# A vision tower on one core: the value-bias product moved behind the repeated values, the engines' order changed at the first LayerNorm and the gates, expert 1 split during attention

## The reference

```python
h = (tokens - mean) * rsqrt(var + eps) * gamma + beta; h = h @ w + b   # patches of 5 shifted images
n = layernorm(h)
q, k, v = n @ qkv_w.T + qkv_b                  # 12 heads of 16
a = softmax(where(mask, q @ k.T / 4, -inf))    # keys j % 8 == 0, j == i, j == i - 1, all causal
h = h + (a @ v) @ out_w.T + out_b
n = layernorm(h)
top_w, top_i = top_k(softmax(n @ router_w.T), 2)
h = h + sum_e gate_e * (gelu(n @ w1[e] + b1[e]) @ w2[e] + b2[e])   # 8 experts, hidden width 768
```

## Time and profile before

| | us |
|---|---|
| median of 3 runs | 223.51 (223.41 to 223.8) |
| profiled execution, its own time | 224.47 |
| its span, first to last instruction | 222.7 |
| PE busy | 193.5 (87%) |
| DVE busy | 139.2 (62%) |
| ACT busy | 115.8 (52%) |
| POOL busy | 78.5 (35%) |

### The profile page before, as it was taken

How to read it: one execution, slowest core, us unless ns; L and a number is a source line. 1 busy time by engine, 2 the same in 40 slices (tenths; PEclk the granted TensorE clock), 3 DMA queues, 4 the chain that set the end, 5 groups by cost and what they waited for, 6 DMA issues and landing times.

```text
span 222.7 us, 3426 instructions
## 1 busy us (share of the span) xinstructions
PE 193.5 (87%) x1124; PEld 169.9 (76%) x1124; DVE 139.2 (62%) x304; ACT 115.8 (52%) x204; POOL 78.5 (35%) x90
## 2 busy tenths in 40 slices
PE   0899988854899958878869999999999999999991
PEld 0898578743897734767759889898998989999981
DVE  4299875747422877645992766466674665756544
ACT  2297642121313123128953767968678696784620
POOL 7781006214400064110841543635436344460000
PEclk9996996955559995559996999999999999999999
DMA  6999992000530000000016008053160520000002
GB/s 139 250 306 294 225 249 53 0 0 0 150 102 0 0 0 0 0 4 0 0 55 195 0 10 236 0 143 104 31 216 0 167 80 0 0 3 0 0 0 74
DMA packets 13930, 17.20 MB, mean 77 GB/s; under 512 B 2303, under 2 KB 10112, under 8 KB 13918
## 3 DMA queue, kind: packets, MB, share of 16 engines
q1 hardware_dynamic: 13374, 17.02, 28.3%
q10 hardware_dynamic: 544, 0.03, 0.2%
HBM read 16.66 MB, written 0.39 MB: 77 GB/s over the span
## 4 chain that ended last, share of the span: by engine, by line
PE 62%; DVE 15%; SPq 8%; issue 6%; DMA 4%; ACT 3%; POOL 1%; DVEq 0%; ACTq 0%; POOLq 0%
PE ps L367 30%; PE ps L1072 15%; PE ps L1074 7%; DMA stage<-in_L_ffn_w 4%; DVE big_r L1138 3%; SPq L398 2%; DVE oh L1138 2%; PE ps L915 2%; DVE norm L1297 1%; PE ps L959 1%; PE ps L804 1%; ACT big_r L328 1%; SPq L352 1%; DVE shifted L1142 1%; POOL rs L512 1%
## 5 line engine op out<-in xcount | busy, mean ns | idle before, releaser
L367 PE MATMUL ps<-big_r,wsplit 128*128 128x512 f32 (+1 forms) x250 | 64.6, 395 | 0.0
L1138 DVE TENSOR_TENSOR big_r<-early,big_r 128x512 fp32r<-128x512 f32 x48 | 45.7, 957 | 26.1 <-ACT big_r L328 25.2
L1072 PE MATMUL ps<-wsplit,big_r 128*128 128x384 f32 x192 | 57.6, 359 | 2.6 <-DVE big_r L1138 2.6
L367 PEld LDWEIGHTS ps<-big_r,wsplit 128*128 128x128 f32 x250 | 44.3, 195 | 6.8
L1074 PE MATMUL ps<-wsplit,big_r 128*128 128x192 f32 x192 | 48.4, 252 | 0.0
L720 ACT ACTIVATE early<-ps,b1t 128x512 f32<-128x512 f32 x48 | 32.7, 682 | 29.6 <-PE ps L367 29.6
L1072 PEld LDWEIGHTS ps<-wsplit,big_r 128*128 128x128 f32 x192 | 36.4, 190 | 5.3 <-DVE big_r L1138 3.5
L1074 PEld LDWEIGHTS ps<-wsplit,big_r 128*128 128x128 f32 x192 | 36.8, 192 | 1.4
L328 ACT ACTIVATE big_r<-early 128x512 fp32r<-128x512 f32 x48 | 30.5, 635 | 1.5
L1487 DVE SCALAR_TENSOR_TENSOR t_a<-ps,gates,merge 128x192 f32<-128x192 f32 x32 | 11.8, 409 | 15.1 <-PE ps L1074 15.1
L310 POOL TENSOR_TENSOR wsplit<-stage,wsplit 128x768 fp32r<-128x768 f32 x4 | 7.4, 1843 | 31.3 <-DVE wsplit L1138 16.3
(11 more groups left out here) (220 smaller groups left out, 292.4 us busy)
## 6 DMA issues: line engine op xcount, KB each, us to landing
stage<-in_L_ffn_w SPq DMA_DIRECT2D x4, 576.0 KB, 5.6
early<-in_L_ffn_w SPq DMA_DIRECT2D x4, 576.0 KB, 5.6
shifted<-in_L_tok_w SPq DMA_DIRECT2D x6, 288.0 KB, 9.1
early<-in_x SPq DMA_DIRECT2D x3, 512.0 KB, 6.8
stage<-in_L_ffn_w SPq DMA_DIRECT2D x4, 384.0 KB, 3.4
stage<-in_L_ffn_w SPq DMA_DIRECT2D x8, 192.0 KB, 4.3
early<-in_L_ffn_w SPq DMA_DIRECT2D x4, 384.0 KB, 3.4
early<-in_L_ffn_w SPq DMA_DIRECT2D x8, 192.0 KB, 4.4
```

Of the source, the lines that this page charges most:

```text
L367: mm = nc.tensor.matmul(dst, lhs, rhs, start=(n == 0), stop=(n == 4))
L1072: nc.tensor.matmul(ps[:, AB[t], 0:2 * D], g_hi[:, j % NG, tok], w2c, start=(f == 0), stop=False)
L1138: return nc.vector.tensor_tensor(o, a, b, op)
```

## The change

- `NTB` becomes (6, 5): group 0 of the first LayerNorm is transposed into bank 6, whose last reader is the second weight piece, so PE waits there for `s_watlo` 2 in place of 4. The wait for 4 stands behind it, ahead of the Q products.
- The three value-bias products go from ahead of the first transposes to behind `repeated_v(3)`, into bank `ATB[1]`. `const_row` on DVE goes behind `outputs(1)`, and PE waits for it ahead of the transposes of `ao` of group 1. `hb` on POOL goes behind the near values.
- DVE at the first LayerNorm: the last low weight piece ahead of `less_mean(1)`, and `embedding(1)` ahead of `low_parts(0)`. ACT: the high parts of expert 0's W2 behind the high part of group 0. POOL: the low part of expert 0's W2 waits for `s_nlo` 2, the low parts of both groups.
- `strided_scores`: first the four products with 128 rows, then the four with 64.
- Expert 1's weights: ACT takes their high parts between the `previous` and `token_major` copies of attention; POOL makes W1's low parts behind `hb`, ahead of the second LayerNorm's `rstd`, and W2's low part behind it. `pair(0)` is written out ahead of the loop without that split, on ACT and DVE.
- Gates on DVE: `two_largest` ahead of `low_hidden(0, 0)`, `gate_values` behind `low_hidden(0, 3)`.

```diff
-        NTB, QB, KB, VB, SB = (5, 6), 7, 6, (0, 2, 3, 5), (6, 7)
+        NTB, QB, KB, VB, SB = (6, 5), 7, 6, (0, 2, 3, 5), (6, 7)
...
             rstd(0, 1)
+            pool.wait_ge(s_nlo, G)
             split_low_w2(pool, 0, 0)
-            pool.wait_ge(s_row, 1)
...
             near_values(0)
             near_values(1)
+            pool.wait_ge(s_nv, G)
+            pool.wait_ge(s_row, 1)
+            pool.wait_ge(s_h, TT)
+            pool.wait_ge(s_watps, 4)
+            nc.gpsimd.tensor_tensor(hb[:], h[:], const_row[:, :].unsqueeze(1).broadcast_to([P, TT, D]),
+                                    ALU.add).then_inc(s_hb, 1)
+            split_low_w1(pool, 1, 1)
             rstd(1, 0)
             rstd(1, 1)
+            split_low_w2(pool, 1, 1)
...
-            split_low(pool, 1, 1)
...
             previous(0)
+            act.wait_ge(s_emb, G + 1)
+            act.wait_ge(d_stage[1], 16 * STAGE_DMAS)
+            split_high(1, 0)
+            split_high(1, 1)
             token_major(2)
             previous(1)
             token_major(3)
             previous(2)
+            split_high(1, 2)
+            split_high(1, 3)
             previous(3)
...
+            pe.wait_ge(s_watlo, 2)
             transposes(0, n1, s_n, lambda t: t + 1, NTB, s_nt, s_ndup)
+            pe.wait_ge(s_watlo, 4)
+            pe.wait_ge(s_wathi, 5)
...
             repeated_v(2)
             repeated_v(3)
+            pe.wait_ge(d_bqk, 16 * BQK_DMAS)
+            pe.wait_ge(s_prev, TT)
+            for n, (col, part) in enumerate(((0, 0), (0, 1), (1, 2))):
+                mm = nc.tensor.matmul(ps[:, ATB[1], 0:D], bias_v[:, col:col + 1].broadcast_to([P, P]),
+                                      wat[:, part, OUT0:OUT0 + D].bitcast(F32), start=(n == 0), stop=(n == 2))
+            mm.then_inc(s_vbias, 1)
...
+            transposes(0, ao, s_ao, lambda t: t // 2 + 1, ATB, s_at, s_aodup)
+            pe.wait_ge(s_row, 1)
+            transposes(1, ao, s_ao, lambda t: t // 2 + 1, ATB, s_at, s_aodup)
...
             outputs(1)
+            dve.wait_ge(s_vbias, 1)
+            tt(const_row[:], ps[:, ATB[1], 0:D], outb_row[:], ALU.add).then_inc(s_row, 1)
...
+                        if first and slot == 0 and j == LAG:
+                            gate_values()
```

More of the change, by code:

```diff
@@ L678, in _ @@
             high_parts(0, s_nt, NTB, nt, s_nhi)
+            split_high(0, 2)
+            split_high(0, 3)
             last_columns_again(0, 1, n1)
@@ L711, in _, with pair @@
             nc.scalar.activation(table_in[:], neg_half[:, 0:1], ACT.Gelu)
-            def pair(i, last):
+            def pair(i, last, first=False):
                 for j in range(2 * FC):
@@ L723, in pair @@
                     copy(g_hi[:, j % NG], gf[:, j % NG]).then_inc(s_ghi, 1)
-                    if last and slot == 1:
+                    if last and slot == 1 or first and slot == 0:
                         continue
@@ L731, in pair @@
                         split_high(1 - slot, f - 1)
-            with act.Fori(0, E // 2 - 1) as i:
+            pair(0, False, first=True)
+            with act.Fori(1, E // 2 - 1) as i:
                 pair(i, False)
@@ L996, in strided_scores @@
                                      kbd_a[:, b].rearrange("p g j -> p (g j)"), start=True, stop=True)
+                for b in range(4 * g, 4 * g + 4):
+                    tok = slice(b * S, (b + 1) * S)
+                    rows = slice(b % 2 * S, (b % 2 + 1) * S)
+                    c0 = b // 2 % 2 * HEADS * NK
                     mm = nc.tensor.matmul(ps[rows, SB[g], c0 + 64:c0 + 96], qt[0:REM, 1, tok],
@@ L1034, in _ @@
                 mm.then_inc(s_pv, 1)
-            for g in range(G):
-                transposes(g, ao, s_ao, lambda t: t // 2 + 1, ATB, s_at, s_aodup)
+            transposes(0, ao, s_ao, lambda t: t // 2 + 1, ATB, s_at, s_aodup)
+            pe.wait_ge(s_row, 1)
+            transposes(1, ao, s_ao, lambda t: t // 2 + 1, ATB, s_at, s_aodup)
             for g in range(G):
@@ L1314, in _ @@
             normalised(0, 0, h, n1)
+            small_low_parts((3,))
             less_mean(1)
-            small_low_parts((3,))
+            embedding(1)
             low_parts(0, s_nhi, NTB, nt, s_nlo)
-            embedding(1)
             statistics(0, 1, h, s_h, lambda t: t + 1)
             normalised(0, 1, h, n1)
-            dve.wait_ge(s_vbias, 1)
             dve.wait_ge(d_rows, 16 * 2)
-            tt(const_row[:], ps[:, UB, 0:D], outb_row[:], ALU.add).then_inc(s_row, 1)
             low_parts(1, s_nhi, NTB, nt, s_nlo)
@@ L1513, in _ @@
             low_hidden(0, 2)
-            gate_values()
-            with dve.Fori(0, E // 2 - 1) as i:
+            pair(0, False, first=True)
+            with dve.Fori(1, E // 2 - 1) as i:
                 pair(i, False)
```

20 lines of the change are left out of this document (3 added, 17 removed).

## The result

The changed kernel takes 208.09 us (median of 4 runs, 206.31 to 208.92) against 223.46 in the runs beside it, a ratio of 0.930 (95% interval 0.924 to 0.936): 15.4 us less, where 11.0 were forecast, and outside the forecast's range at its low end. The profiled execution took 207.82 us, its span is 206.1 (222.7 before).

A forecast was written before the change was run, and what follows sets the result against it. The prediction saw the winnable time ahead of the expert loop at 121 us, in chained waits and PE's slow clock. Its terms summed to -11.0 us, from a median of 223.51 to 212.5 us, range 209.8 to 216.6.

The forecast's parts named there:

- Scores: Reordering of sixteen short products, twice, while PE is the bound: 0.2 us less, from nothing to 0.4.
- First LayerNorm: Reordered steps and W2's wait let tile 0's products start 5.8 us earlier, bounds 5.0 and 6.3.
- The clock in Q, K, V: PE's clock comes up near the start of tile 0: 3.1 us less, bounds 0 and 3.5.
- Value bias: Its 1.16 us hide in PE's wait for value blocks; `const_row` delays group 1's transposes by 0.15 us (0 to 0.4).
- Expert 1's split: On POOL around the second LayerNorm: W1 adds 0.5 us (bound 1.6), W2 beside the norms 0.75 (0 to 1.5).
- The clock at the router: The wait ahead of the second transposes delays the clock's rise: 0.8 us more, bounds 0 and 1.6.
- Gates: Both PE waits go, 2.6 us, and the slow stretch at 117.2, 1.5 us; bounds together 2.0 and 4.2.
- Rivals 1, 3 and 4: In order: clock no earlier, 215.6 us, chance 0.22; gates keep a wait, 216.6 us, 0.12; attention products slow, 226.1 us, 0.04.
- Rival 2: The clock also stays up from 83 us: 2.5 us less, 210.0 us; chance 0.12.

The follow-up runs named there:

- w2_no_wait: The changed kernel without POOL's wait for both low parts ahead of expert 0's W2: 212.04 us.
- s_new_on_before: The kernel before with the new order of the scores' products and nothing else: 218.28 us against 221.28, ratio 0.982.
- w2_late: The changed kernel with one wait added on POOL, so that expert 1's W2 starts behind the second LayerNorm's last norm: 206.03 us.
- ln_only: The kernel before with the first LayerNorm's edits alone (banks, value bias, `const_row`, `hb`, engine order there): 213.22 us against 222.06, ratio 0.964.
- s_old_order: The changed kernel with the scores' products in the old order, 128 rows and 64 rows in turns: 210.28 us.
- s_halves_in_turn: The changed kernel with scores' products alternating column halves, the number of rows changing at six of seven steps: 209.62 us.
- s_rows_together: The changed kernel with the scores' four 128-row products first, then the four of 64 rows, images in order 0, 2, 1, 3: 207.95 us.
- gates_only: The kernel before with expert 1's split in attention, the new order at the gates and the written-out first pair alone: 218.09 us against 222.06, ratio 0.981.
- filled: The changed kernel with expert 1's W1 low parts ahead of the near values, W2's behind the last norm, and sixteen unread products in PE's waits: 205.32 us.

## Why the prediction was wrong

- **The step that failed is "Scores".** It took the value products as the nearest row, looked for the gain in alternating column halves, and put 0.2 us with an upper end of 0.4. The four orders show that the halves are worth nothing and the change between 128-row and 64-row products 0.20 us each; taken away six times in each of two groups on a stretch where PE is the bound, this is 2.4 us. With the other terms as they came, 0.2 us here would have given 210.3 us, inside the range. The upper bound was wrong as well: it took the pace of products whose shapes do not alternate for that of products whose shapes do, and no row of the scores themselves was read for it: in the trace of the kernel before their sixteen records of 64 and 32 columns took 1.95 us a group, where eight records of 192 columns took 0.87 us for the values at the same clock (80.63).
- **First LayerNorm: right.** -6.0 for -5.8, by the steps named: transposes 2.6 us ahead of the first low part, norms at 0.67. `w2_no_wait` shows 2.2 of it to be W2's wait.
- **The clock in Q, K, V: right in place and size.** -3.2 for -3.1, tile 0 at 1.73 us. In all eleven profiled executions with the new first LayerNorm the stretch is 6.27 to 7.12 us. The prediction put the late rise down to the narrow products. With them moved, and the first LayerNorm as before, the clock was up 2.4 us after tile 0's start in one execution and 5.0 us after it in another; that is in keeping with it and does not prove it. What it does to the whole time is not settled. The 0.4 us kept back for the narrow products was not needed, since their ten took 1.28 us in place of 2.23, a factor of 0.57 as for a tile.
- **Value bias: right.** Its six records took 1.24 us behind the repeated values and the stretch to the probabilities did not grow. `const_row` was to cost 0.15, but the stretch shrank by 0.3. PE's clock explains it: group 1's value products took 0.87 us in place of 1.55. `s_new_on_before` has them at 0.87 too, without a `const_row` behind them, and takes 1.97 us from `outputs(1)` to the first output product, where the changed kernel takes 2.24: `const_row` costs 0.27.
- **Expert 1's split: right in sum.** +1.4 for +1.25. By `w2_late` W2 costs 0.8 (0.75 forecast), and by the 12.6 of `ln_only`, which has `hb` there and no W1, W1 costs the other 0.8 (0.5). The step of two elements was held up until W1's end, the statistics not at all. The Trainium skill's rule that the prediction names, in "SBUF — State Buffer", section "SBUF: two separate sides", has the second engine wait for the whole instruction of the first; the trace agrees for the norms (2.98 us beside W2's 2.64) and for `ve`.
- **The clock at the router: a term that comes or does not.** +0.8 was the middle of 0 and 1.6, and the changed kernel's profiled execution shows 0. The other executions speak for the mechanism all the same. Six of the profiled executions have W2 beside the second norms and so the wait ahead of the second transposes: the changed kernel, `s_old_order`, `s_halves_in_turn`, `s_rows_together`, `gates_only` and `w2_no_wait`. Their stretches are 4.62, 5.99, 6.24, 4.63, 5.03 and 6.05 us, 0.8 above 4.62 in the mean. The ten executions without that wait have 4.59 to 4.68. So the 0.8 was a fair mean, and that it stayed away in the changed kernel's profile was the luck of one execution.
- **Gates: right in kind, 0.8 short.** The 4.9 us are 0.7 beyond the upper bound of 4.2. I summed the idle times of the earlier trace rows, 0.75 and 1.87; start to start, the same steps lose 0.91 and 2.13 against 2.29 us, since the record of a product ends after the next could have begun. The slow stretch cost 1.85, not 1.5, being longer than the window that I read. `gates_only` shows 4.9 for the part by itself, without saying how much of it DVE's order is.
- **What is no effect of the change:** 0.9 us ahead of group 0's norm and 0.2 behind the first `add_expert`. The medians' 15.4 is less than the profiled pair's 16.6 by about that. Rivals 1, 3 and 4 did not come. Rival 2 named a real cost that the change left: `filled` takes 2.3 us out of the stretch.

Summed in the table's order, the misses are -0.9, -0.2, -0.1, -2.2, -0.4, +0.1, -0.8, -0.8 and -0.2, 5.5 us (5.6 from the unrounded starts). The scores are the largest of them and the only one that lies far outside its own bounds.

## What to carry to other kernels

A reordering of small products is not a small edit: look at each step of the list for the number of rows of the stationary tile, and price a change from the trace by start-to-start differences, not by busy time. Before a long POOL instruction is put into an idle place of POOL, ask what DVE does there with operands in SBUF; a W2 cost 2.2 us beside the first norms and 0.8 beside the second, with a later clock behind it in three of six executions, and W1 cost 1.4 beside the near scores. Waits at PE are best summed from start to start, with the slow clock that follows them.
